# Cap and scale of exp(k): from a VectorE instruction into ScalarE's exponent

## The reference

```python
ek  = exp(min(k, 30.0));  ekv = ek * k
a_t = a_{t-1} * decay + ekv_t        # forwards (nf) and backwards (nb)
b_t = b_{t-1} * decay + ek_t         # forwards (df) and backwards (db)
euk = exp(min(u + k, 30.0))
num = nf + nb - ekv + euk * k
den = df + db - ek + euk
y   = sigmoid(x) * num / max(den, 1e-8) * (0.8 + 0.2 * tf)
out = x + y @ (sign(W) * mean|W|).T + bias
```

## Time and profile before

| | |
|---|---|
| median of 3 runs | 518.72 us (518.04 to 519.01) |
| the profiled execution's own time | 518.05 us |
| its span, from first to last instruction | 516.1 us |
| VectorE busy | 492.4 us, 95% |
| ScalarE busy | 392.8 us, 76% |
| GpSimd busy | 382.6 us, 74% |
| TensorE matmul busy | 360.2 us, 70% |

### The profile page before, as it was taken

The page is one execution under the profiler, slowest core; times in us unless marked ns, Lnnn a source line. Parts: engine busy times, 40 slices in busy tenths (PEclk is TensorE's granted clock), DMA queues, the critical chain, the costliest instruction groups (busy, mean ns, idle before and its releaser), DMA issues.

```text
span 516.1 us, 5401 instructions
## 1 busy us (share of the span) xinstructions
PE 360.2 (70%) x1797; PEld 209.0 (41%) x1803; DVE 492.4 (95%) x375; ACT 392.8 (76%) x440; POOL 382.6 (74%) x210
## 2 busy tenths in 40 slices
PE   3323323333497877878877696988759999899995
PEld 2223312332253444444434354454325555454442
DVE  6999999999999999999999999999999999999775
ACT  3969889797949999999969879696877766674500
POOL 0158777778787777787787777877878788989383
PEclk9995555555697978898889898897969999999998
DMA  8776999999988997878889968787777668986069
GB/s 223 185 239 215 269 226 270 276 292 263 264 220 195 204 190 141 161 176 189 177 191 203 198 121 170 178 190 175 152 123 122 103 104 154 166 143 102 6 107 220
DMA packets 101283, 94.22 MB, mean 183 GB/s; under 512 B 2924, under 2 KB 93064, under 8 KB 100744
## 3 DMA queue, kind: packets, MB, share of 16 engines
q0 software_dynamic: 31440, 36.18, 46.6%
q1 hardware_dynamic: 67720, 56.65, 34.2%
q10 hardware_dynamic: 2096, 1.05, 0.8%
HBM read 60.31 MB, written 37.75 MB: 190 GB/s over the span
## 4 chain that ended last, share of the span: by engine, by line
DVE 69%; issue 20%; PE 9%; ACT 0%; DMA 0%; DVEq 0%; SPq 0%
DVE pair L888 26%; DVE pair L902 14%; DVE pair L916 7%; DVE wkv L927 7%; DVE own L917 7%; DVE pair L911 5%; PE prod L486 2%; PE sT L486 2%; PE kT L486 2%; DVE euk L933 1%; PE cols L486 1%; DVE y_start L894 1%; PE yT L486 1%; DMA cond<-in_cond_dram 0%; PE kT L502 0%
## 5 line engine op out<-in xcount | busy, mean ns | idle before, releaser
L445 PE MATMUL prod<-acts,sgn 128*128 128x512 f16 x752 | 188.2, 407 | 7.4 <-ACT orow L795 6.8
L902 DVE TENSOR_TENSOR_SCAN pair<-cols,y_start,pair 128x1024 f32<-128x1024 f32 x64 | 150.1, 2346 | 1.1
L888 DVE TENSOR_TENSOR_SCAN pair<-cols,pair 128x1024 f32<-128x1024 f32 x64 | 142.8, 2272 | 0.0
L445 PEld LDWEIGHTS prod<-acts,sgn 128*128 128x128 f16 x752 | 78.5, 105 | 99.9 <-issue 23.2
L379 POOL TENSOR_TENSOR wkv<-wkv,rec 128x1024 f32<-128x1024 f32 x31 | 73.4, 2368 | 35.7 <-ACT wkv L740 35.5
L370 POOL TENSOR_TENSOR wkv<-euk,rec 128x1024 f32<-128x1024 f32 x31 | 79.1, 2552 | 22.9 <-ACT rec L685 22.9
L420 PE MATMUL kT<-ident,k_nat 128*128 128x128 f32 x248 | 44.4, 338 | 69.3 <-DVE own L917 69.3
L390 POOL TENSOR_TENSOR wkv<-wkv,pair 128x1024 f32<-128x1024 f32 x31 | 73.1, 2358 | 10.4 <-DVE wkv L927 10.1
L683 ACT ACTIVATE rec<-euk,lnb 128x1024 f32<-128x1024 f32 x31 | 35.6, 1149 | 48.5 <-DVE euk L933 48.5
L337 POOL TENSOR_TENSOR acts<-wkv,rec 128x1024 f16<-128x1024 f32 x30 | 71.4, 2379 | 0.2 <-ACT rec L694 0.2
L420 PEld LDWEIGHTS kT<-ident,k_nat 128*128 128x128 f32 x248 | 36.4, 176 | 76.7 <-issue 75.8
(11 more groups left out here) (117 smaller groups left out, 574.6 us busy)
## 6 DMA issues: line engine op xcount, KB each, us to landing
pair<-own POOLq DMA_DIRECT2D x32, 512.0 KB, 4.6
out_dram<-in_x_dram SPq DMA_DIRECT2D x32, 512.0 KB, 6.3
k_nat<-in_fside_BxSxS_dram SPq DMA_DIRECT2D x30, 512.0 KB, 4.6
x_nat<-in_x_dram SPq DMA_DIRECT2D x26, 512.0 KB, 6.1
out_dram<-o_nat POOLq DMA_DIRECT2D x24, 512.0 KB, 6.3
y_fm<-in_L_ffn_weight_dram SPq DMA_DIRECT2D x8, 512.0 KB, 6.4
out_dram<-in_L_ffn_bias_dram POOLq DMA_DIRECT2D x8, 512.0 KB, 8.7
x_end<-in_x_dram SPq DMA_DIRECT2D x6, 512.0 KB, 7.1
```

Source lines behind the costliest of these rows:

```text
L445: ins = pe.matmul(made_in(u), view[:, c, m % CT * P:m % CT * P + P], acts[:, part, m // CT % 2 * CT + c, h * H:(h + 1) * H], start=(part = ...
L888: dve.tensor_tensor_scan(buf, d, buf, 0.0, ALU.mult, ALU.add).then_inc(st["F" + kind], 1)
L902: dve.tensor_tensor_scan(buf[:, ::-1], d, buf[:, ::-1], y_start[:, i:i + 1], ALU.mult, ALU.add)\
```

## The change

For all steps but the first, ScalarE makes the capped and scaled exponential itself: relu(30 - k) first, then exp(-that + capped), where capped = 30 + ln(scl) (with a first-order correction of the logarithm through iscl). VectorE's clamp stays only for n = 0. Two small activations and two small VectorE operations in step 0 make `capped`. GpSimd's store waits for val of its step in place of the clamp. The VectorE's scan of ek waits for nothing of its own engine any more, the scan of ekv for val. NO goes from 5 to 4.

```diff
-    NO = 5
+    NO = 4
@@ gpsimd step
-                    done(pool, "clamp", n)
+                    done(pool, "val", n)
                     store(ready[0])
@@ scalar exps(n, p)
                 done(act, "kT", n)
                 done(act, "den", n - 2)
-                act.activation(ek[p], kT[:, :], ACT.Exp).then_inc(st["expE"], 1)
+                act.activation(ek[p], kT[:, :], ACT.Relu, scale=-1.0, bias=cap[:, 0:1]).then_inc(st["below"], 1)
+                act.wait_ge(s_capped, 1)
+                done(act, "below", n - 1)
+                act.activation(ek[p], ek[p], ACT.Exp, scale=-1.0, bias=capped[:, n:n + 1]).then_inc(st["expE"], 1)
                 act.activation(euk[p][:, :], kT[:, :], ACT.Exp, bias=ucol[:, n:n + 1])\
                    .then_inc(st["expU"], 1)
@@ scalar, before the steps
+            act.wait_ge(s_scl, 1)
+            act.activation(lscl[:, :], scl[:, :], ACT.Ln).then_inc(s_lscl, 1)
+            act.wait_ge(s_lscl, 1)
+            act.activation(iscl[:, :], lscl[:, :], ACT.Exp, scale=-1.0).then_inc(s_lscl, 1)
@@ vector
+            def caps():
+                dve.wait_ge(s_lscl, 2)
+                link(dve.tensor_tensor(iscl[:, :], iscl[:, :], scl[:, :], ALU.mult))
+                dve.scalar_tensor_tensor(capped[:, :], iscl[:, :], CAP - 1.0, lscl[:, :], ALU.add, ALU.add)\
+                   .then_inc(s_capped, 1)
@@ vector step n
                 done(dve, "expE", n)
+                if n == 0:
+                    dve.tensor_scalar(E, E, E30, scl[:, 0:1], ALU.min, ALU.mult).then_inc(st["clamp"], 1)
+                    shares()
+                    done(dve, "clamp", 0)
                 done(dve, "base", n - 2)
-                dve.tensor_scalar(E, E, E30, scl[:, n:n + 1], ALU.min, ALU.mult).then_inc(st["clamp"], 1)
-                if n == 0:
-                    shares()
-                done(dve, "clamp", n)
                 done(dve, "expU", n)
                 dve.tensor_tensor(V, E, kT[:, :], ALU.mult).then_inc(st["val"], 1)
                 dve.scalar_tensor_tensor(own[p][:, :], U, E30, kT[:, :], ALU.min, ALU.mult)\
                    .then_inc(st["own"], 1)
-                forward(E, n, "clamp", "d")
-                forward(V, n, "val", "n")
+                if n == 0:
+                    caps()
+                forward(E, n, "d")
+                done(dve, "val", n)
+                forward(V, n, "n")
```

More of the change, by code:

```diff
@@ L30 @@
 E30 = 10686474581524.463
+CAP = 30.0
 DEN_MIN = 1e-8
@@ L147, in bi_wkv_binary_ffn @@
         tiny = sb("tiny", [P, 1])
+        cap = sb("cap", [P, 1])
+        lscl = sb("lscl", [P, N])
+        iscl = sb("iscl", [P, N])
+        capped = sb("capped", [P, N])
         kT = ps("kT", [P, T])
@@ L167, in bi_wkv_binary_ffn @@
         k_first = [sem(f"k_first{i}") for i in range(NH)]
-        s_head = sem("s_head")
+        s_head, s_scl, s_lscl, s_capped = (sem(a) for a in ("s_head", "s_scl", "s_lscl", "s_capped"))
         o_out = [sem(f"o_out{p}") for p in range(NO)]
@@ L176, in bi_wkv_binary_ffn @@
         st = {a: sem("d_" + a) for a in (
-            "kT", "expE", "expU", "sig", "sT", "clamp", "val", "own", "Fd", "Fn", "starts", "yd", "yn", "den",
+            "kT", "below", "expE", "expU", "sig", "sT", "clamp", "val", "own", "Fd", "Fn", "starts", "yd", "yn", "den",
             "ln", "rec", "chk", "two", "inv", "gate", "base", "hi", "hib", "lo",
@@ L633, in _ @@
         def _(act):
-            seed(act, "expE", "expU", "sig", "ln", "rec", "two", "hi", "hib", "ev", "yc", "abs", "sgn", "wTc")
+            seed(act, "below", "expE", "expU", "sig", "ln", "rec", "two", "hi", "hib", "ev", "yc", "abs", "sgn", "wTc")
             for i in range(NH):
@@ L699, in early_out @@
                 act.copy(park[i], park_bank[i]).then_inc(st["early_sb"], 1)
-            act.wait_ge(s_const, 4)
+            act.wait_ge(s_const, 5)
             act.wait_ge(s_ucol, 2)
@@ L852, in _ @@
             dve.memset(tiny[:, :], TINY).then_inc(s_const, 1)
+            dve.memset(cap[:, :], CAP).then_inc(s_const, 1)
             dve.wait_ge(s_cond, 16)
@@ L874, in _ @@
             link(dve.scalar_tensor_tensor(scl[:, :], dec[:, :], 1.0, onem[:, :], ALU.add, ALU.mult))
-            link(dve.tensor_scalar(scl[:, :], scl[:, :], S_MIN, None, ALU.max))
+            dve.tensor_scalar(scl[:, :], scl[:, :], S_MIN, None, ALU.max).then_inc(s_scl, 1)
+            dve.wait_ge(s_scl, 1)
             link(dve.tensor_copy(dec_ps, dec[:, :]))
@@ L883, in shares, with forward @@
                                   ALU.mult, ALU.add).then_inc(s_gain, 1)
-            def forward(buf, n, after, kind):
-                done(dve, after, n)
+            def caps():
[3 more added lines that the diff above has]
+                   .then_inc(s_capped, 1)
+            def forward(buf, n, kind):
                 d = dec_ps[:, n:n + 1].to_broadcast([P, T])
```

## The result

| | before | changed |
|---|---|---|
| median | 518.50 us (518.04 to 519.01, 4 runs) | 530.87 us (530.74 to 532.63, 4 runs) |
| the profiled execution | 518.05 | 530.91 |
| its span | 516.1 | 528.9 |
| ratio | | 1.0246, 95% interval 1.0222 to 1.0270 |

The account below looks back on a forecast made before the run. VectorE's own instructions were taken to set the pace, with ScalarE's load mattering step by step. The 23.9 us saving was almost entirely given back as stalls ahead of the gate: +2.9, 521.6 us, range 516.8 to 525.5.

Parts of the forecast that it names:

- What VectorE saves: Without the clamp, VectorE's step floor falls from 14.71 to 13.94 us, 0.77 less, 23.9 us over 31 steps.
- What ScalarE pays: One exponential becomes a relu and a dependent exponential, 2.20 us in place of 0.90, 1.30 us more per step.
- The stall ahead of the gate: VectorE waits for inv when L683 is late; steps 12 to 16 stall 1.52 us, period 15.46, +0.75 each.
- Steps 2 to 7: Pairs: even steps run at 13.94 (-0.77), odd ones stall 1.98 us (+1.22); three times, +1.35 in all.
- Step 17: With lo ahead of inv, inv ends 9.66 us after L683; stall 2.29 us, +1.52.
- The store's wait: Store waiting for val delays chk by 0.48 us; stalls of 0.23 in steps 28 to 30, 0.17 in step 24.
- Four buffers: One output buffer less costs nothing, as each y_copy comes at least 3 us after its awaited store lands.
- TensorE's products: Waits for products in steps 18 to 23 taken as slack, adding nothing to that stretch's sum of -0.77 us.
- The one for +6: Rival: the store's wait lags twice as much, or TensorE's products come later; +6, 524.6 us, chance 0.14.
- steps 18 and 26 at 13.94: Sign expected in the changed profile: these two steps should last 13.94 us.
- a stall of 1.5 us in steps 12 to 16: Sign expected in the changed profile: VectorE idles about 1.5 us ahead of the gate there, waiting for inv.
- a stall ahead of val: Sign against the forecast: it is wrong if the stall comes ahead of val; no size given.

Follow-up runs that it names:

- the saving alone: Changed kernel with ScalarE's old single exponential back, clamp still left out after step 0, den as it is: 518.32 us, 1.0007 of the kernel before.
- the price alone: Changed kernel with relu and exponential kept on ScalarE, but VectorE's clamp back in every step and the store waiting for it: 531.30 us, 1.0246.

## Why the prediction was wrong

The sign was right, the size was not: +12.4 against +2.9. The sign is not luck: with den's standing still out of the way the changed kernel still takes 1.0108 of the kernel before, 5.9 us more. Less the 2.4 of the late kT and the 0.9 behind step 31 this is 2.6, close to the 2.9: ScalarE's stalls do outweigh the clamps.

- **What VectorE saves** is the step that failed, in the words "the floor of a step falls to 14.71 - 0.77 = 13.94 us". Val does start where the clamp did, and the gate is wanted at 9.29. But the 4.64 us from the gate to the next step were carried over from the kernel before as if they belonged to VectorE alone. They hold den, which does not run beside base; and base keeps its place, fixed by GpSimd's chain L685, chk, L740, inv, lo, base, when VectorE moves 0.77 ahead. Before, they overlapped by 0.14 us; now by 0.95 or 1.09. A punctual step is base's end plus 1.0: 13.73 + 1.01 = 14.74. The three steps 18, 20, 22 lasted 14.75, 14.76 and 14.88 in place of 13.94, steps 26 and 27 14.74 and 14.75. The saving, forecast at 23.9 us, was worth nothing by itself (518.32 against 518.17), and 14.6 us once den had one SBUF input (503.55).
- **What ScalarE pays** held. The pair took 1.20 + 1.06 = 2.26 us, 1.36 more than the old one (1.30 forecast); other starts on the queue moved by a little less, so that steps 12 to 14 lasted 15.49 (15.46).
- **The stall ahead of the gate** was right in kind, but the gate came 0.59 us late in steps 12 to 14, not 1.52. Den's 0.94 took up the rest: where ScalarE sets the pace of each step in a row, den's standing still costs nothing further. With den on one SBUF input the gate starts at 10.78 in step 12, 1.49 after it is wanted, as forecast (1.52).
- **Steps 2 to 7** came out at 14.15, 16.72, 14.02, 16.71, 14.04, 16.69. The odd ones are the forecast 15.93 and some 0.8 for den. **Step 17** took 14.94 in place of 16.23: its L691 came only 0.95 after the start, and base, with lo ahead of inv, ends early.
- **The store's wait** was right where L740 waits for chk (steps 28 to 30 0.14, 0.29 and 0.14 us ahead of the gate, step 24 0.21; 0.23 and 0.17 were forecast), but it has a second price there, since it moves base as well. Four buffers: right, nothing.
- **TensorE's products** "taken as slack": right in the changed kernel, where den holds VectorE up for longer than TensorE is late; wrong by 2.4 us once den is out of the way.
- **The rivals.** None named den. The one for +6, a dearer store or later products, had the right direction only. Of the signs on record two failed, steps 18 and 26 at 13.94 and a stall of 1.5 us in steps 12 to 16. The sentence on what would show it wrong, a stall ahead of val, looked at the wrong sign: there is no stall to be seen, the time is inside an instruction.

In sum, from the steps: steps 1 to 30 took 11.5 us more than forecast (5.3 of it in steps 24 to 30, 2.7 in steps 2 to 7, 2.6 in steps 18, 20 and 22); step 31 and what follows took 1.2 less, and a stumble of 0.36 in step 20 of the kernel before did not come back; 11.5 - 1.2 - 0.4 = 9.9, the difference between the spans' 12.8 and 2.9.

The Trainium skill has the rule, on the page "SBUF — State Buffer", Who interferes with whom: a VectorE instruction with two SBUF inputs contends with a GpSimd instruction that reads SBUF, while one with at most one SBUF input, outside the modes that use both pairs of ports, does not; the shared ports are an exclusive lock, and the order of issue decides who is blocked. The traces agree, but for the first 0.14 us of the overlap, which cost nothing: 2.17 us at an overlap of 1.09, 1.22 with an input moved to PSUM. Den first and base second no run here shows; for another pair the changed kernel's L992 and L402 show that order, and there GpSimd's instruction is the one that gets longer, 1.75 for 1.27.

## What to carry to other kernels

Before counting on a shorter engine, list which of its instructions share something with another engine, and ask where that other engine's instruction lies after the shift; an order that looks slack may be what keeps the two apart. A busy share, or a list of waits, does not show an instruction that stands still: compare the mean duration of each group before and after, and look in the old trace for instructions of one group that last longer at one place than at another (L969 here). And where one saving moves the meeting point of two chains, test the saving alone and the price alone; here they were worth 0 and 12.4 us, and in the kernels that leave nothing out the saving counted almost only where the other chain was shorter (L740 earlier, the store's wait out of it).

## What the runs showed of the hardware

Den (scalar_tensor_tensor, 128x1024 f32, both inputs in SBUF) stood still for the whole of its overlap with GpSimd's tensor_tensor but the first 0.14 us (1.23 to 2.17 us). In the other order it was GpSimd's tensor_tensor (128x512 f32, inputs in SBUF) that lasted longer: 1.75 us in place of 1.27, after VectorE's L992 had begun 0.06 us ahead of it. VectorE's scans, own and gate, each with one input in SBUF and the other in PSUM, kept their 2.27 and 2.35, 1.21 and 1.19 to 1.22 us beside GpSimd's instructions (own beside chk in the kernel before); val never lay beside one. A DMA issue on GpSimd beside den (0.90 us of it in step 13 of the kernel before) cost den nothing. The relu out of PSUM with a bias took 1.11 us and brought no table load.
